# Expert weights copied in two halves, with a longer ring and a new request order in the last group

## What is computed

```python
# attention part, on x = LayerNorm(x) of shape (8, 512, 128), added to x
xa = ln(x, g0, b0);  xs = shift(xa)                       # one token later
k, v = mix(xa, xs, tm_k) @ Wk, mix(xa, xs, tm_v) @ Wv
r = sigmoid(mix(xa, xs, tm_r) @ Wr)
x = x + (r * wkv(w, u, k, v)) @ Wo                        # wkv: a decaying scan over 512 tokens
xc = ln(x, g1, b1)
x = x + sigmoid(mix(xc, xs) @ Wcr) * (square(relu(mix(xc, xs) @ Wck)) @ Wcv)
# second part, on x = LayerNorm(x), added to x
q, k, v = h @ Wq, h @ Wk, h @ Wv                          # 16 heads of 8
x = x + (softmax(q k^T / sqrt(8)) v) @ Wo
m = ln(x, g2, b2)
wts, idx = top_k(softmax(m @ Wg), 2)                      # 2 of 8 experts, weights made to sum to 1
ye = gelu(m @ W1[e] + b1[e]) @ W2[e] + b2[e]              # 128 -> 512 -> 128
x = x + sum over the two experts of wts * ye
```

## Time and profile before

| | us |
|---|---|
| median of 3 runs | 981.62 |
| lowest, highest | 976.5, 984.49 |
| the profiled execution | 989.37 |
| its span, first to last instruction | 987.7 |
| busy in the span: PE, DVE, ACT, POOL | 820.5, 665.6, 600.2, 424.9 |

### The profile page before, as it was taken

How to read it: one execution, slowest core, us unless ns; L and a number is a source line. 1 busy time by engine, 2 the same in 40 slices (tenths; PEclk the granted TensorE clock), 3 DMA queues, 4 the chain that set the end, 5 groups by cost and what they waited for, 6 DMA issues and landing times. The chain is left out here.

```text
span 987.7 us, 15981 instructions
## 1 busy us (share of the span) xinstructions
PE 820.5 (83%) x5416; PEld 516.9 (52%) x5416; DVE 665.6 (67%) x1341; ACT 600.2 (61%) x1016; POOL 424.9 (43%) x543
## 2 busy tenths in 40 slices
PE   3558898878898999788989998988898888898772
PEld 1444445434555654345556555654565555478771
DVE  4538858886879688868886878687867576223112
ACT  2123446644787687447876887677768876556341
POOL 5544333534553455464534553454556013115263
PEclk9675798888899999898999999998999998699797
DMA  6500321991522300015233321053223320558793
GB/s 196 169 12 9 122 98 49 292 347 45 179 90 89 101 21 9 12 33 180 89 100 103 108 86 57 30 183 97 89 80 123 119 80 27 181 188 298 236 309 95
DMA packets 106286, 116.77 MB, mean 118 GB/s; under 512 B 7983, under 2 KB 89310, under 8 KB 106206
## 3 DMA queue, kind: packets, MB, share of 16 engines
q1 hardware_dynamic: 102110, 107.36, 34.3%
q0 software_dynamic: 4096, 8.40, 2.6%
HBM read 77.24 MB, written 38.49 MB: 117 GB/s over the span
## 5 line engine op out<-in xcount | busy, mean ns | idle before, releaser
L1456 DVE TENSOR_REDUCE QA<-psB 128x2 f32<-128x1024 f32 x256 | 311.9, 1219 | 124.0 <-PE psB L1143 121.7
L943 ACT ACTIVATE PT<-psB 128x1024 f32<-128x1024 f32 x256 | 261.9, 1023 | 134.3 <-PE psB L1159 130.4
L1159 PE MATMUL psB<-Q,KT 32*128 32x512 f32 x512 | 134.4, 521 | 34.0 <-ACT PT L943 20.6
L1143 PE MATMUL psB<-KT,Q 24*128 24x512 f32 x512 | 136.9, 530 | 22.6 <-DVE QA L1456 21.7
L1171 PE MATMUL psV<-PT,VA 128*32 128x512 f32 x1024 | 148.5, 654 | 0.6
L1236 PE MATMUL psA<-MX,WB 128*128 128x128 f32 x792 | 109.4, 290 | 31.2 <-ACT H L971 19.7
L971 ACT ACTIVATE H<-psA,WB 128x128 f32<-128x128 f32 x396 | 109.8, 376 | 33.3 <-PE psA L1236 31.3
L1236 PEld LDWEIGHTS psA<-MX,WB 128*128 128x128 f32 x792 | 100.0, 202 | 39.4 <-issue 28.3
L1246 PEld LDWEIGHTS psY<-WB,H 128*128 128x128 f32 x792 | 96.8, 194 | 27.8 <-ACT H L971 16.8
L1159 PEld LDWEIGHTS psB<-Q,KT 32*128 32x128 f32 x512 | 49.7, 191 | 117.1 <-ACT PT L943 75.3
L1246 PE MATMUL psY<-WB,H 128*128 128x128 f32 x792 | 107.6, 282 | 0.0
(11 more groups left out here) (198 smaller groups left out, 1360.0 us busy)
## 6 DMA issues: line engine op xcount, KB each, us to landing
WB<-w_rows SPq DMA_DIRECT2D x99, 578.0 KB, 5.7
pairs<-XT SPq DMA_DIRECT2D x2, 5120.0 KB, 18.5
outs<-XT SPq DMA_DIRECT2D x2, 5120.0 KB, 33.5
XT<-pairs SPq DMA_DIRECT2D x99, 64.0 KB
outs<-YT SPq DMA_DIRECT2D x99, 64.0 KB
w_rows<-WB SPq DMA_DIRECT2D x8, 578.0 KB, 3.3
X<-in_L_attn_x_dram SPq DMA_DIRECT2D x8, 256.0 KB, 3.0
H<-in_L_ffn_W_dram SPq DMA_DIRECT2D x8, 256.0 KB, 3.9
```

The source lines that it names most:

```text
L943: act.activation(PT[:, (c % 2) * G + j:(c % 2) * G + j + 2, :], psT, ACT.Exp, scale=SCALE).then_inc(t_taken.sem, 1)
L1143: pe.matmul(dst[:, h, :], chunk(Q1[r, g, :], c), KT[r, g, :], start=True, stop=True).then_inc(s_full.sem, 1)
L1159: pe.matmul(psT[:, h, :], chunk(KT[r, g, :], c), Q2[r, g % 2, :], start=True, stop=True).then_inc(t_full.sem, 1)
L1456: dve.tensor_reduce(QA[:, c, g * G + j:g * G + j + 2, RM], plain(b, i), AX_X, ALU.max).then_inc(s_taken.sem, 1)
```

## The change

1. A weight row is now W1, b1, W2, b2, and is copied in two halves: `first_layer_in` (516 columns) and `second_layer_in` (640), on semaphores of their own (`w1_in`, `w2_in`). The first half waits, tile by tile, until GELU has emptied the bank of the tile that holds the ring entry; the second, as before, for `y_taken`. TensorE's second layer waits for `w2_in`.
2. Buffers of head and tail (EE, MK, MV, MR, K, V, R, EV, D, PP, AA) become one tensor LATE, and six more ring entries WX lie over it. In the last group the windows go through four places instead of two: windows 29, 30 and 33 use WX, windows 31 and 32 WB. So windows 29 to 32 wait for none of windows 29 to 32.
3. In the last group `begin` looks up the table first, then asks for the first halves, then waits for the scatter and reads the rows, then asks for the second halves. In the other groups rows come first.
4. SP's steps move: next rows at slot 7 (was 3), first halves at 9 and second at 10 (was 7), write-back at 15 (was 9), begin at 1 and 3 (was -4 and 0), stores at 30 and 45 after a group's end (were 40 and 41).
5. The tables of the other engines and USES get new slots. The instructions are the same; their order in the streams changes by neighbours.

```diff
--- before.py
+++ after.py
@@ -110,7 +110,7 @@
     WINDOWS = [-(-tiles // WIN) for tiles in TILES]
     TILE_0 = [sum(TILES[:group]) for group in range(GROUPS)]
     WINDOW_0 = [sum(WINDOWS[:group]) for group in range(GROUPS)]
-    W2, B1, B2 = F, 2 * F, 2 * F + NF
+    B1, W2, B2 = F, F + NF, 2 * F + NF
...
-        D = sb("D", [P, T])
-        MK = sb("MK", [P, T])
-        MV = sb("MV", [P, T])
-        MR = sb("MR", [P, T])
-        K = sb("K", [P, T])
-        V = sb("V", [P, T])
-        R = sb("R", [P, T])
-        PP = sb("PP", [P, T + 1])
-        EE = sb("EE", [P, 4, T])
-        EV = sb("EV", [P, T])
-        AA = sb("AA", [P, T + 1])
+        WR = 2 * F + NF + C
+        LATE = sb("LATE", [P, 12 * T + 2 * (T + 1)])
+        EE = LATE[:, 0:4 * T].rearrange("p (a t) -> p a t", a=4)
+        MK, MV, MR, K, V, R, EV, D = (LATE[:, i * T:(i + 1) * T] for i in range(4, 12))
+        PP = LATE[:, 12 * T:13 * T + 1]
+        AA = LATE[:, 13 * T + 1:14 * T + 2]
+        WX = LATE[:, 0:2 * WIN * WR].rearrange("p (r n) -> p r n", n=WR)
...
@@ -388,12 +385,24 @@
             first = (w - WINDOW_0[group]) * WIN
             return range(TILE_0[group] + first, TILE_0[group] + min(first + WIN, TILES[group]))
 
+        def home(w):
+            late = w - WINDOW_0[GROUPS - 1]
+            return w % 2 + (2 if late >= 0 and late % 4 < 2 else 0)
+
         def ring(n):
-            return window(n) % 2 * WIN + within(n) % WIN
+            return home(window(n)) * WIN + within(n) % WIN
+
+        def ring_rows(r, size=1):
+            return WB[:, r:r + size, :] if r < 2 * WIN else WX[:, r - 2 * WIN:r - 2 * WIN + size, :]
+
+        def weights_of(n):
+            return ring_rows(ring(n))[:, 0, :]
 
         def landed(n):
-
-            return 16 * sum(within(n) % WIN < len(members(w)) for w in range(window(n) % 2, window(n) + 1, 2))
+            return 16 * sum(within(n) % WIN < len(members(w)) for w in range(window(n) + 1) if home(w) == home(window(n)))
+
+        def holder(w):
+            return max([v for v in range(w) if home(v) == home(w)], default=None)
 
         def moved(w):
...
@@ -525,10 +534,19 @@
 
             blocks, experts = {}, {}
 
+            def look_up(w):
+                group = window_group(w)
+                if w == WINDOW_0[group]:
+                    sp.wait_ge(map_ready.sem, map_ready.at(group, 1))
+                for n in members(w):
+                    if n not in blocks:
+                        i = within(n)
+                        both = sp.value_load(TMAP[i:i + 1, group % 2:group % 2 + 1], min_val=0, max_val=E * (BLOCKS - 1) - 1)
+                        blocks[n], experts[n] = both >> 3, both & (E - 1)
+
             def rows_in(w):
                 group = window_group(w)
                 if w == WINDOW_0[group]:
-                    sp.wait_ge(map_ready.sem, map_ready.at(group, 1))
                     for k in range(2):
                         for c in range(NT):
                             sp.wait_ge(scattered[k][c], 16 * (MEMBERS[group][-1] + 1))
@@ -538,20 +556,26 @@
                 if w >= 2:
                     u = use(members(w - 2)[0], "x")
                     sp.wait_ge(u.taken, u.after)
+                look_up(w)
                 for n in members(w):
                     i = within(n)
-                    both = sp.value_load(TMAP[i:i + 1, group % 2:group % 2 + 1], min_val=0, max_val=E * (BLOCKS - 1) - 1)
-                    blocks[n], experts[n] = both >> 3, both & (E - 1)
                     sp.dma_start(XT[:, w % 2, i % WIN, :], XS[group % 2].rearrange("(b p) n -> b p n", p=P)[blocks[n]]).then_inc(xt_in[w % 2], 16)
 
-            def weights_in(w):
+            def first_layer_in(w):
                 if w == 0:
                     for e in range(E - 4, E):
                         sp.wait_ge(w_out[e % 4], 16 * (e // 4 + 1))
-                if w >= 2:
-                    sp.wait_ge(y_taken.sem, y_taken.at(w - 2, 1))
+                for i, n in enumerate(members(w)):
+                    if holder(w) is not None:
+                        u = use(members(holder(w))[min(i, len(members(holder(w))) - 1)], "h")
+                        sp.wait_ge(u.taken, u.after)
+                    sp.dma_start(weights_of(n)[:, 0:W2], WS[experts[n]][:, 0:W2]).then_inc(w1_in[ring(n)], 16)
+
+            def second_layer_in(w):
+                if holder(w) is not None:
+                    sp.wait_ge(y_taken.sem, y_taken.at(holder(w), 1))
                 for n in members(w):
-                    sp.dma_start(WB[:, ring(n), :], WS[experts[n]]).then_inc(w_in[ring(n)], 16)
+                    sp.dma_start(weights_of(n)[:, W2:], WS[experts[n]][:, W2:]).then_inc(w2_in[ring(n)], 16)
 
...
@@ -571,9 +595,13 @@
                 if goes_on(n):
                     rows_in(window(n) + 2)
 
-            def next_weights(n):
+            def next_first(n):
                 if goes_on(n):
-                    weights_in(window(n) + 2)
+                    first_layer_in(window(n) + 2)
+
+            def next_second(n):
+                if goes_on(n):
+                    second_layer_in(window(n) + 2)
...
@@ -584,8 +612,13 @@
 
             def begin(i):
                 def step(group):
+                    if group == GROUPS - 1:
+                        look_up(WINDOW_0[group] + i)
+                        first_layer_in(WINDOW_0[group] + i)
                     rows_in(WINDOW_0[group] + i)
-                    weights_in(WINDOW_0[group] + i)
+                    if group < GROUPS - 1:
+                        first_layer_in(WINDOW_0[group] + i)
+                    second_layer_in(WINDOW_0[group] + i)
                 return step
 
             def keep(which):
@@ -594,9 +627,10 @@
                         store(MEMBERS[group][which])
                 return step
 
-            TILE = {3: (tile_step(0, next_rows),), 7: (tile_step(0, next_weights),), 9: (tile_step(0, rows_out),)}
-            GROUP = {-4: (begin(0),), 0: (begin(1),)}
-            END = {40: (keep(0),), 41: (keep(1),)}
+            TILE = {7: (tile_step(0, next_rows),), 9: (tile_step(0, next_first),), 10: (tile_step(0, next_second),),
+                    15: (tile_step(0, rows_out),)}
+            GROUP = {1: (begin(0),), 3: (begin(1),)}
+            END = {30: (keep(0),), 45: (keep(1),)}
...
@@ -820,13 +854,13 @@
                     pool.indirect_dma_start(YG[:, b % 2, c, k, :], None, YS[group % 2],
                                                 bass.IndirectOffsetOnAxis(IDX[:, b % 6, k, c:c + 1], 0)).then_inc(gathered[k][c], 16)
 
-            HEAD = {21: (head_norm,), 22.5: (head_shift,), 28: (head_sigmoid,)}
-            TAIL = {0: (side, wkv_out, wkv_sum,), 5: (norm_1, tail_shift,), 8.5: (residual,), 10.5: (square,), 11: (sigmoid,),
-                    19: (norm_2,), 31.5: (residual_2,)}
-            CORE = {8: (keep,)}
-            POST = {6: (c_norm,), 16: (positions, scatter(0),), 21: (scatter(2),)}
-            END = {4: (gather(0, 0),), 8: (gather(0, 1), gather(0, 2),), 16: (gather(0, 3),), 17: (gather(1, 0),),
-                   31: (gather(1, 1),), 32: (gather(1, 2), gather(1, 3),)}
+            HEAD = {25.5: (head_norm, head_shift,), 30.5: (head_sigmoid,)}
+            TAIL = {1.5: (side,), 2: (wkv_out,), 8.5: (wkv_sum, norm_1, tail_shift,), 10.5: (residual,), 16.5: (square,),
+                    17.5: (sigmoid,), 22.5: (norm_2,), 31.5: (residual_2,)}
+            CORE = {11: (keep,)}
+            POST = {9: (c_norm,), 17.5: (positions,), 22: (scatter(0),), 23: (scatter(2),)}
+            END = {9: (gather(0, 0),), 10: (gather(0, 1),), 12: (gather(0, 2), gather(0, 3),), 22: (gather(1, 0),),
+                   38: (gather(1, 1),), 40: (gather(1, 2),), 44: (gather(1, 3),)}
...
-                act.wait_ge(w_in[ring(n)], landed(n))
+                act.wait_ge(w1_in[ring(n)], landed(n))
                 for f in range(NF):
                     last = act.activation(H1[:, n % 4, f, :], use(n, "h").bank[:, f * TW:(f + 1) * TW],
-                                          ACT.Gelu_apprx_tanh, bias=WB[:, ring(n), B1 + f:B1 + f + 1])
+                                          ACT.Gelu_apprx_tanh, bias=weights_of(n)[:, B1 + f:B1 + f + 1])
                 last.then_inc(use(n, "h").taken, 1)
...
@@ -1229,33 +1263,35 @@
             def hidden(n):
                 i = within(n) % WIN
                 pe.wait_ge(use(n - i, "x").taken, use(n - i, "x").after)
-                pe.wait_ge(w_in[ring(n)], landed(n))
+                pe.wait_ge(w1_in[ring(n)], landed(n))
                 u = use(n, "h")
                 pe.wait_ge(u.taken, u.before)
                 for f in range(NF):
-                    last = pe.matmul(u.bank[:, f * TW:(f + 1) * TW], WB[:, ring(n), f * P:(f + 1) * P],
+                    last = pe.matmul(u.bank[:, f * TW:(f + 1) * TW], weights_of(n)[:, f * P:(f + 1) * P],
                                      MX[:, window(n) % 2, i, :], start=True, stop=True)
                 last.then_inc(u.full, 1)
 
```

(36 more changed lines are left out.)

35 lines of the change are left out of this document (18 added, 17 removed).

## The result

The changed kernel takes 992.62 us (median of four runs, 988.48 to 997.22) against 982.35 us (976.5 to 984.49) for the kernel before, measured beside it: a ratio of 1.009 with a 95% interval of 1.0053 to 1.0128. It is slower by 9 us by the ratio (10.3 us between the two medians) where 4 us of gain were forecast, and the time lies above the range.

What follows compares the result with a forecast made beforehand. Attention was taken as bound by TensorE and its hand-written order, the last windows by SP's issuing. Nothing for the tables and 4.0 us off the last eviction took the median from 981.62 to 977.6 us, range 967 to 988.

Steps and rivals of the forecast that it cites:

- The retimed tables: Seven attention turns: neighbouring steps swap; no gain or loss taken.
- The bound of 5 us: Uncertainty kept for the retimed tables: 5 us either way over seven attention turns.
- The halves: Weight copies: doubled issues add 1.8 us of SP per window; no change taken up to the last group.
- The queue laid out from 8.5 us a window: SP's issue order from window 22 on; in the last group its last issue comes 0.5 us later.
- SP is the bound: Rival: late SP loses the 3.0 us in front and windows follow its 8.5 us pace; 988.4 us, chance 0.17.
- Its first condition: SP-bound rival: SP reaches window 29's first halves more than 0.8 us later, after the scatter, losing 3.0 us.
- its second: SP-bound rival: windows 23 to 27 follow SP at 8.5 us instead of 7.35, costing 5.8 us.
- Weights before rows: Start of last group: rows land 1.53 us after their issue; transposes at 923.7, first layer at 924.8.
- The last eviction: Window 33: first half issued at 955.9, landing 5.7 us, then 3.85 us; eviction at 965.5 against 969.49, 4.0 us gained.
- What follows the last eviction: Write-back, eight gathers, combine and store at the end: unchanged, moving along with the last eviction.
- The ring: Last group: windows 29 and 30 no longer wait for 27 and 28; window 29's first layer starts 3.0 us sooner.
- The rival built on cheap issues: SP's issues overlap with waits: last four windows at TensorE's 6.8 us, 5.9 us gained plus 3.0; 972.7 us, chance 0.13.

Runs made afterwards that it cites:

- e1: Kernel before with the change's new tables of PE, ACT, DVE and POOL and its USES only: 990.49 us, ratio 1.0054.
- e8: Kernel before with the new tables of POOL and VectorE only, on a slower chip: 1023.27 us, ratio 1.0004.
- e13: Kernel before with the changed kernel's order of PE and ACT and its USES only: 991.28 us, ratio 1.0073.
- e11: Kernel before with each tile's table entry looked up twice by SP, no copy changed: 992.37 us, ratio 1.0099.
- e10: Kernel before with each expert's weights copied in two halves and nothing else, on a slower chip: 1030.04 us, ratio 1.0069.
- e12: Kernel before with weights copied in two halves only, run again on another chip: 987.65 us, ratio 1.0043.
- c0: The kernel before, unchanged, run again for a second profile: 986.28 us, ratio 1.0027.
- c1: The kernel before, unchanged, run again for a later profile: 982.47 us.
- e3: Changed kernel, but rows asked for ahead of the first halves in the last group too: 991.51 us, ratio 1.008.
- e2: Changed kernel with the old tables of PE, ACT, DVE and POOL; halves, ring, request order and SP's table new: 987.93 us, ratio 1.0023.
- e7: Changed kernel with all five engines at their old slots, SP included; halves and ring kept: 984.83 us, ratio 1.0025.
- e9: Kernel before with the ring of twelve and early look-ups in the last group, whole copies, on a slower chip: 1023.51 us, ratio 1.0003.
- e6: Changed kernel with old tables of the four engines and whole weight copies; ring, early look-ups and SP's table new: 987.97 us, ratio 1.0049.

## Why the prediction was wrong

**The retimed tables failed, and by most.** "I take nothing, nearest to the size of a single wait row." Measured: 0.54% (0.24 to 0.83) for all four tables (e1), 5.3 us, and 0.73% (0.29 to 1.17) for PE and ACT alone. The bound of 5 us that stood beside it was right in size; the value in the middle was not. The term had been put at nothing because no row named a gain, and the error was to judge a swap by PE's wait rows. One step that the timelines show to cost is an ACT step, moved out of idle time into the one stretch of a turn in which ScalarE is full, 0.49 us; the rest of what a turn loses is not traced to a step. The earlier trace rows couldn't show that; ScalarE's timeline around its two table loads would have. Of the 3.7 us in the fourth turn the prediction had nothing either: POOL's new slots and the new order of PE and ACT, neither of which does it alone (e8, e13), put a two-input VectorE step under four POOL squares. In the medians this does not show: e13, without it, loses no less than e1, with it.

**The halves were mis-sized in what they take.** The queue laid out from 8.5 us a window seems to hold to the decimal: rows of window 33 forecast until 954.1, issued until 954.11; w1 955.9 against 956.69; w2 957.7 against 958.24. That is luck. The scatter landed 4.1 us sooner than laid out (916.1 against 920.23), but SP was still issuing window 29's first halves (915.98 to 917.68), so the rows went out only 2.3 us sooner (until 919.65 against 922.0); then it lost the 2.3 us, 34.5 us from window 29's rows to window 33's where 32.1 had been laid out, without waiting for anything. The step that failed is the one that read this queue as harmless because its last issue comes only 0.5 us later (it came 1.1 us later, 958.24 against 957.15). With no slack left, whatever delays SP delays the landings behind it; that is a reading, and e11 is the run that bears it out. e10 and e12 put the halves alone at 0.69% (0.31 to 1.07) and 0.43% (0.23 to 0.63), 4 to 7 us; e11 reproduces at least as much with SP's time alone. The rival "SP is the bound" had the mechanism and the side, and the whole change lies nearer to its 988.4 us than to the forecast. Its first condition came true, SP arrived at the rows 1.6 us or more after the scatter; its second did not: windows 23 to 27 stay at 7.30 us, the cost comes behind window 31.

**Weights before rows: the landing.** "The last lands as before, 1.53 us after its issue ends." It was 4.25 us. The rest of the step held: with rows issued by 919.65 instead of 922.0, SP being 2.3 us earlier than laid out, the transposes came at 923.90 against 923.7 forecast and the first layer at 925.35 against 924.8. Two errors hid each other. The 1.53 us was no accident of one profile: wherever rows are asked for first it is 1.5 to 1.7 us (c0 1.57, c1 1.54, e3 1.72, e12 1.60). It was the change of order that undid it. Window 33's rows too took 4.12 us from the end of their issue to the transposes (954.11 to 958.23), with other copies keeping the engines full.

**The last eviction.** Forecast 965.5, measured 967.73. Window 33's first layer began at 959.68; at full clock, 3.4 us, it would have been through 1.9 us sooner than with the 5.33 us that it took at 0.50. That is 1.9 of the 2.2 us. The prediction had taken the clock as unchanged. Before, window 33's last eight matmuls ran at full clock, 1.13 us; now the window follows a wait of 2.5 us for its rows.

**What follows the last eviction.** It was to be "unchanged", a term put at nothing. It takes 19.0 us instead of 18.2, and 18.9 to 19.1 us in every kernel with halves (e2, e3, e7, e10, e12), 18.8 us in e11, 18.1 to 18.4 us in all others. SP's last write-back takes 1.6 us to issue instead of 1.3 and the first gather starts 0.7 us later. No run shows why.

**The ring** was to give the 3.0 us in front. The eviction of window 29 comes 9.6 us behind window 28's instead of 11.8, but that is so because window 28's is 5.2 us late; from the landing of the scatter to the first layer of window 29 it is 9.2 us (916.1 to 925.35) where it was 7.5 (920.23 to 927.77; 8.0 us in c0). In the median the ring is worth nothing alone (e9, 1.0003, 0.9965 to 1.004). It may take back a part of what the halves cost: halves 1.0043 and 1.0069, halves with ring 1.0023 and 1.0025, with intervals that overlap.

**The sum.** Forecast: 0 - 4.0 us. Measured by parts: + 5.3 (tables) + 2.3 (the rest), 7.6 us, where the whole change measured 9 with an interval of 5 to 13. The rival built on cheap issues gives 972.7 us. It is what the Trainium skill, "DMA: Bandwidth & Descriptors", section "Issuing engines are not separate DMA queues", would make of it, by its rule that the time to initiate a DMA is usually small beside the DMA; in this kernel e11 speaks against it: SP's time alone, with no copy changed, gives 1.0099.

What stays open: why e1, with the old copies, loses less behind the scatter in its profile (46.6 us to the last eviction, e13 48.6); how much of the halves' cost is packets (the 1.2 us of e12 above e11 in the last group are less than the 1.6 us by which two profiles of the kernel before differ), which steps of PE's and ACT's new order cost what, and what e9, which is e6 with the write-back early again, makes of the last group on a chip like the first ones: its only profile is of the slower chip. No kernel here beats the one before; e9 can't be told from it.

## What to carry to other kernels

Count the issuing engine's time per round as you count TensorE's, and look at how long it waits: when splitting copies takes that wait to nothing, later landings can pay, although no engine looks busier. Before moving a step by half a slot, look at the timeline of the engine that runs it at the new place, not at the waits of the busiest engine; a step of 0.6 us was free in idle time here and cost 0.49 us in a full stretch, once a turn. Look also at what a mark waits for before you measure a stretch from it: window 28's eviction had moved by 5.2 us behind a combine. Compare medians and stretches at equal clock, since one profiled execution can lie 0.8% from its median by a single clock dip.

## What the runs showed of the hardware

- A VectorE operation with two SBUF inputs took 0.19 us with no POOL operation beside it, 0.72 us when it started 0.36 us into one POOL tensor operation (until that one's end), and 4.19 us beside four back-to-back ones (until the last one's end; 1.22 us in e8, where it started 2.9 us after the first, until the same end).
- A small read behind 0.8 MB of weights was used 4.25 us after the end of its issue, against 1.5 to 1.7 us without them.
- A second look-up of a register from SBUF costs SP 0.56 us: three rows with doubled look-ups take 3.74 us from first to last issue (e11) where they took 2.63.
- A packet more for the same bytes took 18 to 22 ns of engine time (pages of before and after, c1 and e12, e9 and e10), where a line through two queues had given 4 ns. For the 1920 packets of the last group that would be an estimated 2.4 us over 16 engines in place of 0.5.
- One chip ran the kernel before 4% slower (1022.93 us), with a granted clock of 0.88 to 0.90 where the other chips had 0.90 to 0.93; the ratio of the halves kept its sign there (1.0069, and 1.0043 elsewhere).
